# An RWKV block in f32: the LoRA products of four mixes as one group of four row tiles, their mixes in two groups, and new hand orders

## The chip, the core and the metric

The kernel runs on one core of a Trainium2 chip, all in 32-bit floats. The metric is the device time of one execution in microseconds (us), as the median of several runs. A core has TensorE (PE, matrix products into PSUM), VectorE (DVE), ScalarE (ACT), GpSimd (POOL) and SyncE (SP, here only for starting DMAs), each with its own queue of instructions that run in order; they wait for one another by semaphores. PSUM has eight banks of 512 floats in each of 128 partitions.

## The reference

64 sequences of 64 tokens with 256 features, one RWKV-6 block with 32 heads of size 8:

```
xn = layernorm(x);  sx = previous token's xn - xn
t  = tanh((xn + sx*maa_x) @ maa_w1)            # 256 -> 5 groups of 32
x5[n] = xn + sx*(maa[n] + t[n] @ maa_w2[n])    # five mixes: k, w, v, r, g
k, v, r = x5[k]@Wk.T, x5[v]@Wv.T, x5[r]@Wr.T;  g = silu(x5[g]@Wg.T)
w = exp(-exp(time_decay + tanh(x5[w]@decay_w1) @ decay_w2))
per token:  a = k (x) v;  out = r . (u*a + s);  s = a + w*s      # s is 8 x 8 a head
x = x + (groupnorm(out) * g) @ Wo.T
xn2 = layernorm(x);  xk, xr = xn2 + (previous - xn2)*ffn_maa
x = x + sigmoid(xr@ffn_Wr.T) * (relu(xk@ffn_Wk.T)**2 @ ffn_Wv.T)
```

## The kernel before, in words

The 64 sequences are cut into nine chunks, of 4, 6, then six times 8, then 6 sequences (256, 384, 512 ... 384 tokens); features lie on partitions, in two halves of 128, and tokens on the free axis. The last chunk's second half of the block is done in three parts, called 8, 9 and 10. The work of a chunk is cut into named steps, for each engine some:

- Norm and shift: `st`, `nrm` (ACT), `rd1` (POOL, a power), `T1` (PE, transposes into `pa`), `xn` (ACT), `shift` (DVE: sx and the input of the first LoRA product).
- LoRA: `W1` (PE, into `pb`), `th` (ACT, tanh), then the mixes. The first four groups of 32 rows of `th` hold the mixes k, w, v, r; mix n = 0, 1, 2, 3 is v, k, w, r, so each reads its own 32 rows of `th` and of `w2`. `X01` is the products of n = 0 and 1, both halves (`lora_half`, four products with 32 rows to contract), into `pa` and `pb`; `mix0` and `mix1` (DVE) turn them into x5. `X2` is the first halves of n = 2 and 3, into `pb`, `X3` the second halves into the same banks, so X3 waits for `mix2`, the step that reads X2; `mix3` reads X3. `X4` and `mix4` are the gate's.
- A mix is `mix_half` once for each half (L459, (product + maa) * sx) and then the addition of xn (L468, `add_xn`, on DVE), or, from chunk 2 on and for n = 1, 3, 4, an adding DMA that POOL starts (`ad1`, `ad3`, `ad4`, L363).
- Projections on PE into `pa`: `P0` (v), `P1` (k), `P3` (r), `P4` (g), each eight passes in L843 (a 32-bit product is two passes); `D1`, `D2` (decay), `CB` (L965, the bonus). ACT empties them: `v`, `k`, `thd`, `r`, `w`, `tg`.
- v goes to DRAM (`vst`, SP) and comes back repeated on the partitions (`vl0`, `vl1`, SP).
- Scan, four times q = 0 to 3: `a`q (L524, k*v), POOL's `s0`q (start state, L394), `sc`q (four scans, L534), `rs`q (times r, L542), PE's `S`q (sums into `patt`, L984, four 32-column tiles). `kv` has two buffers, so a(q) waits for S(q-2).
- Out: `BO` (L975, the bonus into `patt`), `sq` (ACT), `VR` (PE, L996), `rstd` (ACT), `gate` (DVE, L552 and L558), `WO` (PE, L850), `res` (DVE, L567), `st2`, `rd2` (POOL, L384), `nrm2`, `T2` (PE, L835), `xn2` (ACT, L792), `shift2` (DVE, L595 to L600: sx, then xr, then xk), `RR` (L850), `rr` (ACT), `KK` (L843), `kk` (ACT, L812 and L814), `Y2` (L850), `out` (DVE, L610), `ay` (POOL, an adding DMA into the output, L403). `lx` loads x, `lr` loads it again for the residual, `sx2` stores.

Each engine runs its steps in an order written out by hand, `DVE_ORDER` and so on: a pair (name, lag) stands for that step of chunk i - lag in round i; the rounds' end is replaced by a tail that names every step (`DVE_TAIL` ...). In the middle of the span DVE scans chunk c while it mixes chunk c+1 and does `gate` and `res` of chunk c-1. In DVE's order before, one round has

```
rk.1 a0.1 shift.2 bonus.1 sc0.1 gate.0 rs0.1 mix0.2 mix1.2 res.0 a1.1 a2.1 mix2.2
sc1.1 mix3.2 rs1.1 shift2.0 mix4.2 sc2.1 a3.1 rs2.1 sc3.1 rs3.1 rk.2 out.0 a0.2
```

Of the kernel before, what the change touches and what calls it, by code (L numbers as in the profile page):

```python
# [99 lines left out]


def build(nc, x, prev, s0, vecs, w1, w2, dw1, dw2, large, consts, out):

    vscr = nc.dram_tensor("v_scratch", [2, E * T], F32, kind="Internal").ap()
    with ExitStack() as ctx:
# [307 lines left out]
        def _(dve):
# [56 lines left out]
            def a_mix(c, p, n):  # L470

                dve.wait_ge(x_done, 4 * c + (4 if n == 4 else 1))
                if n == 4:

                    dve.wait_ge(pv_done, c + 1)
                elif c >= 1:
                    dve.wait_ge(pg_done if n == 0 else pk_done, c)
                src = pa if n == 0 else pb
                for a in range(HF):
                    ins = mix_half(c, n, a, src[:, a])  # L480
                ins.then_inc(mixed, 1)
                add_xn(c, n)

            def a_mix_pair(c, p, a):

                dve.wait_ge(x_done, 4 * c + 2 + a)
                if a == 0 and c >= 1:
# [3 lines left out]
                mix_half(c, 2, a, pb[:, 0])
                mix_half(c, 3, a, pb[:, 1]).then_inc(mixed, 1)
                if a == HF - 1:
                    add_xn(c, 3)

            def a_rk(c, p):
                dve.wait_ge(r_ready, c + 1)
                dve.wait_ge(k_ready, c + 1)

                dve.wait_ge(x_done, 4 * (c + 1))  # L500
# [593 lines left out]
```

## Time and profile before

| | |
|---|---|
| median of three runs | 539.96 us (539.35 to 544.64) |
| the profiled execution | 541.4 us, span 539.6 us |
| mean granted clock of TensorE | 0.918 of full |
| DVE busy | 482.4 us, 89% of the span |
| PE busy | 460.1 us (85%) |
| ACT, POOL busy | 284.3 us (53%), 91.2 us (17%) |
| 0 to 50 us | DVE busy 21.93 |
| 272 to 330 us (a full chunk) | DVE busy 57.43, PE 54.16 |
| 500 to 539.6 us | DVE busy 20.94 |

The span is the time from the first to the last instruction of the profiled execution; some time lies around it. A row of the timeline gives start, length, engine, line and operation, what it writes and reads, how many instructions are merged into it, and in brackets the engine's idle time before it with what ended that.

### The profile page before, as it was taken

What the parts mean: (1) busy time and instruction counts of PE and PEld (TensorE: products, weight loads), DVE (VectorE), ACT (ScalarE), POOL (GpSimd) and SP (SyncE); (2) the same over time, 40 slices, a digit from 0 to 9 for tenths busy, and PEclk for the clock granted to TensorE, in tenths of its full rate; (3) what the DMA queues carried; (4) which work ended last, traced back from release to release, by engine and by line L of the source; (5) the groups of instructions that cost most, each with busy time, mean ns of one, the idle gap of its engine ahead of it and who ended that gap; (6) DMA issues with size and microseconds to landing.
All of it is one profiled execution on the core that took longest, in us unless ns stands there. A gap on an engine that the chain in (4) does not pass through costs nothing.

```text
span 539.6 us, 5791 instructions
## 1 busy us (share of the span) xinstructions
PE 460.1 (85%) x1968; PEld 257.4 (48%) x1968; DVE 482.4 (89%) x530; ACT 284.3 (53%) x614; POOL 91.2 (17%) x93
## 2 busy tenths in 40 slices
PE   0786889899799988999799979999899969954857
PEld 0463554464356344654365436544465536532435
DVE  0457999999999999989999999999999999999474
ACT  5353177378526844665636852765456263633533
POOL 0001011211420041010332042113202121101020
PEclk9996989899989996998899988999799979985888
DMA  8271291688377827980798357772796069711020
GB/s 267 95 193 21 84 223 30 155 200 187 61 183 162 188 40 171 205 199 2 139 211 207 67 79 182 171 183 54 159 223 151 2 126 226 153 40 30 0 39 30
DMA packets 26726, 69.34 MB, mean 129 GB/s; under 512 B 1608, under 2 KB 19656, under 8 KB 24264
## 3 DMA queue, kind: packets, MB, share of 16 engines
q1 hardware_dynamic: 19448, 54.55, 40.6%
q0 software_dynamic: 7248, 14.42, 15.8%
q8 instruction: 16, 0.26, 0.2%
q14 instruction: 14, 0.11, 0.1%
HBM read 46.15 MB, written 12.19 MB: 108 GB/s over the span
## 4 chain that ended last, share of the span: by engine, by line
PE 51%; issue 22%; DVE 11%; ACT 9%; POOL 5%; DMA 1%; SPq 0%; DVEq 0%; ACTq 0%; POOLq 0%
PE pa L843 13%; PE pc L850 10%; PE pc L843 4%; PE patt L984 4%; PE pb L910 3%; POOL out L403 2%; PE pc L835 2%; PE pb L953 2%; DVE kv L534 2%; DVE x L459 2%; PE pa L881 2%; PE pa L938 2%; POOL rs L384 1%; ACT ob L673 1%; PE pb L869 1%
## 5 line engine op out<-in xcount | busy, mean ns | idle before, releaser
L534 DVE TENSOR_TENSOR_SCAN kv<-w_sb,kv 128x512 f32<-128x512 f32 (+2 forms) x144 | 147.1, 1083 | 0.1
L843 PE MATMUL pa<-x,large_sb 128*128 128x512 f32 (+2 forms) x288 | 129.2, 596 | 2.2 <-DVE x L468 1.7
L843 PEld LDWEIGHTS pa<-x,large_sb 128*128 128x128 f32 x288 | 59.0, 212 | 62.4 <-issue 49.4
L542 DVE TENSOR_TENSOR kv<-kv,r_sb 128x2048 f32<-128x2048 f32 (+2 forms) x36 | 73.7, 2048 | 0.4
L524 DVE TENSOR_TENSOR kv<-vrep,k_sb 128x2016 f32<-128x2016 f32 (+2 forms) x36 | 71.8, 2012 | 0.2 <-PE patt L984 0.2
L394 POOL COPY kv<-s_sb 128x32 f32<-128x32 f32 (+2 forms) x36 | 34.6, 963 | 189.8 <-PE patt L984 171.5
L881 PE MATMUL pb<-th,w_sb 32*128 32x512 f32 (+2 forms) x108 | 40.8, 681 | 18.7 <-DVE x L459 18.7
L459 DVE SCALAR_TENSOR_TENSOR x<-pb,vec_sb,sx 128x512 f32<-128x512 f32 (+2 forms) x72 | 46.1, 681 | 7.0 <-PE pb L881 4.8
L363 POOL DMA_DIRECT2D x<-xn x21 | 19.7, 936 | 177.9 <-DVE x L459 177.9
L639 ACT ACTIVATE ob<-xres 128x256 f32<-128x256 f32 x29 | 11.7, 405 | 52.1 <-DVE xres L567 52.1
L984 PE MATMUL patt<-kv,const_sb 128*32 128x512 f32 (+2 forms) x288 | 36.4, 578 | 0.1
L850 PE MATMUL pc<-large_sb,xr 128*128 128x256 f32 x120 | 30.8, 411 | 2.9 <-DVE xr L600 2.9
L850 PE MATMUL pc<-large_sb,att 128*128 128x256 f32 x120 | 29.2, 397 | 4.2 <-DVE att L558 4.2
L850 PEld LDWEIGHTS pc<-large_sb,xr 128*128 128x128 f32 x120 | 23.9, 205 | 13.2 <-DVE xr L600 5.0
L804 ACT ACTIVATE trr<-pc 128x1024 f32<-128x1024 f32 (+3 forms) x9 | 7.9, 881 | 41.9 <-PE pc L850 41.9
L850 PEld LDWEIGHTS pc<-large_sb,att 128*128 128x128 f32 x120 | 24.0, 201 | 12.0 <-DVE att L558 5.7
L850 PE MATMUL pc<-large_sb,sq 128*128 128x256 f32 x120 | 28.3, 387 | 0.5 <-ACT sq L814 0.4
L843 PE MATMUL pc<-xk,large_sb 128*128 128x512 f32 (+3 forms) x72 | 28.1, 533 | 0.4 <-ACT trr L804 0.4
L881 PEld LDWEIGHTS pb<-th,w_sb 32*128 32x128 f32 x108 | 13.2, 211 | 31.3 <-DVE x L459 25.3
L850 PEld LDWEIGHTS pc<-large_sb,sq 128*128 128x128 f32 x120 | 22.1, 190 | 9.8 <-issue 5.7
L835 PE MATMUL pc<-const_sb,ob 128*128 128x128 f32 x60 | 14.3, 409 | 13.4 <-ACT ob L673 13.4
L730 ACT ACTIVATE k_sb<-pa 128x1024 f32<-128x1024 f32 (+2 forms) x9 | 8.4, 928 | 32.2 <-PE pa L843 32.2
(128 smaller groups left out, 779.3 us busy)
## 6 DMA issues: line engine op xcount, KB each, us to landing
vrep<-v_scratch SPq DMA_DIRECT2D x12, 2048.0 KB, 13.7
x<-xn POOLq DMA_DIRECT2D x18, 512.0 KB, 7.4
vrep<-v_scratch SPq DMA_DIRECT2D x4, 1536.0 KB, 10.7
x_tok<-in_x SPq DMA_DIRECT2D x6, 512.0 KB, 9.6
v_scratch<-v_sb SPq DMA_DIRECT2D x12, 256.0 KB
xres<-in_x SPq DMA_DIRECT2D x6, 512.0 KB, 4.2
out<-xres SPq DMA_DIRECT2D x6, 512.0 KB, 13.9
out<-trr POOLq DMA_DIRECT2D x6, 512.0 KB, 7.0
```

Of the source, the lines that this page charges most:

```text
L363: pool.dma_start(x5[:, x5_slot(n), :, 0:nt], xn[:, c % 2, :, 0:nt], accum_op=ALU.add).then_inc(x5_added[n], 16)
L394: pool.tensor_copy(kv[:, q % 2, :, 0:nb, 0], s0_sb[:, half, G4 * j:G4 * (j + 1), FIRST[c]:FIRST[c] + nb]).then_inc(s0_put, 1)
L459: return dve.scalar_tensor_tensor(out=x5[:, x5_slot(n), a, 0:nt], in0=src[:, 0:nt], scalar=vec(f"maa{g}", a), in1=sx[:, a, 0:nt], op0=ALU. ...
L524: dve.tensor_tensor(kv[:, q % 2, :, 0:nb, 1:L], vv[:, G4 * j:G4 * (j + 1), :, 0:L - 1], kk, ALU.mult).then_inc(kv_ready, 1)
L534: ins = dve.tensor_tensor_scan(flat, w_sb[:, p, q % HF, 0:nb].rearrange("p b t -> p (b t)"), flat, 0.0, ALU.mult, ALU.add)
L542: dve.tensor_tensor(flat, flat, r_sb[:, p, q % HF:q % HF + 1, 0:n].broadcast_to([P, G4, n]), ALU.mult).then_inc(rs_ready, 1)
L835: ins = pe.transpose(dst[:, a, i * P:(i + 1) * P], src[:, t, a * P:(a + 1) * P], ident)
L843: ins = pe.matmul(dst[:, m, 0:n], w(a)[:, m * P:(m + 1) * P], src[:, a, :], start=(a == 0), stop=(a == HF - 1))
L850: ins = pe.matmul(product_tok(k)[:, i], src[:, a, t * P:(t + 1) * P], w(a), start=(a == 0), stop=(a == HF - 1))
L881: return pe.matmul(dst[:, 0:nt], w2_sb[rows, a * P:(a + 1) * P], th[rows, 0, 0:nt], start=True, stop=True)
L910: ins = pe.matmul(pb[:, a, f * nf:(f + 1) * nf], w24_sb[:, f, a * P:(a + 1) * P], th[:, 1, 0:nf], start=True, stop=True)
L984: ins = pe.matmul(patt[d * H:(d + 1) * H, j, 0:n], sum_k[:, half, :], kv[:, q % 2, d, 0:nb].rearrange("p b t -> p (b t)"), start=False, st ...
```

## The change

The products of n = 0 to 3 are issued together, one half of the features at a time: `XA` the first halves, `XB` the second, each four products in four row groups, into the four banks `pa[:, 0]`, `pa[:, 1]`, `pb[:, 0]`, `pb[:, 1]`. DVE's `mixA` reads all four first halves, `mixB` the second halves, with the additions of xn. XB waits until mixA has read the banks; P0, which writes `pa`, waits for the second halves of n = 0 and 1; mixA waits until P4, P1, D1 and P3 of the chunk before are done with. The orders and tails of all five engines are new, and each now has a head, written out. In the middle DVE's round becomes

```
rk.1 rs3.0 a0.1 out.-1 shift.2 bonus.1 sc0.1 gate.0 mixA.2 rs0.1 mixB.2 res.0
a1.1 a2.1 sc1.1 mix4.2 rs1.1 shift2.0 sc2.1 a3.1 rs2.1 sc3.1
```

and PE's goes from `W1 X01 BO WO S0 P0 X2 X3 T2 P1 X4 S1 RR D1 KK D2 P3 S2 Y2 T1 S3 CB VR P4` to `W1 XA BO XB WO S0 P0 X4 P1 T2 S1 D1 RR P3 KK D2 S2 Y2 T1 S3 CB VR P4`.

```diff
-PE_ORDER = [("X01", 1), ("BO", 2), ("WO", 3), ("S0", 2), ("P0", 1), ("X2", 1), ("X3", 1), ("T2", 3), ("P1", 1),
-            ("X4", 1), ("S1", 2), ("RR", 3), ("D1", 1), ("KK", 3), ("D2", 1), ("P3", 1), ("S2", 2), ("Y2", 3),
-            ("T1", 0), ("S3", 2), ("CB", 1), ("VR", 2), ("P4", 1), ("W1", 0)]
-POOL_ORDER = [("s02", 3), ("s03", 3), ("ad4", 2), ("s00", 2), ("ad0", 1), ("s01", 2), ("ad1", 1), ("rd1", 0),
-              ("ay", 4), ("rd2", 3), ("ad3", 1)]
-SP_ORDER = [("vl1", 4), ("vst", 3), ("lx", 1), ("vl0", 3), ("sx2", 5), ("lr", 4)]
+DVE_ORDER = [("a2", 3), ("sc1", 3), ("mix4", 2), ("rs1", 3), ("shift2", 4), ("sc2", 3), ("a3", 3), ("rs2", 3),
+             ("sc3", 3), ("rk", 2), ("rs3", 3), ("a0", 2), ("out", 4), ("shift", 1), ("bonus", 2), ("sc0", 2),
+             ("gate", 3), ("mixA", 1), ("rs0", 2), ("mixB", 1), ("res", 3), ("a1", 2)]
+PE_ORDER = [("W1", 1), ("XA", 1), ("BO", 2), ("XB", 1), ("WO", 3), ("S0", 2), ("P0", 1), ("X4", 1), ("P1", 1),
+            ("T2", 3), ("S1", 2), ("D1", 1), ("RR", 3), ("P3", 1), ("KK", 3), ("D2", 1), ("S2", 2), ("Y2", 3),
+            ("T1", 0), ("S3", 2), ("CB", 1), ("VR", 2), ("P4", 1)]
+POOL_ORDER = [("ay", 4), ("ad3", 1), ("rd1", 0), ("rd2", 3), ("ad4", 1), ("s03", 2), ("s00", 1), ("ad0", 0),
+              ("ad1", 0), ("s01", 1), ("s02", 1)]
+SP_ORDER = [("sx2", 7), ("vl1", 5), ("lr", 6), ("vst", 4), ("vl0", 4), ("lx", 2)]
...
-DVE_TAIL = [("rs1", 7), ("shift2", 6), ("a3", 7), ("sc2", 7), ("mix4", 8), ("rs2", 7), ("sc3", 7), ("rs3", 7),
-            ("rk", 8), ("out", 6), ("a0", 8), ("sc0", 8), ("gate", 7), ("bonus", 8), ("a1", 8), ("rs0", 8),
-            ("res", 7), ("sc1", 8), ("a2", 8), ("rs1", 8), ("sc2", 8), ("rs2", 8), ("shift2", 7), ("a3", 8),
-            ("sc3", 8), ("rs3", 8), ("gate", 8), ("gate", 9), ("out", 7), ("gate", 10), ("res", 8), ("st2", 8),
+DVE_TAIL = [("rs1", 7), ("mix4", 8), ("shift2", 6), ("a3", 7), ("sc2", 7), ("rs2", 7), ("sc3", 7), ("rs3", 7),
+            ("rk", 8), ("out", 6), ("a0", 8), ("a1", 8), ("sc0", 8), ("gate", 7), ("rs0", 8), ("sc1", 8),
+            ("bonus", 8), ("rs1", 8), ("res", 7), ("a2", 8), ("sc2", 8), ("a3", 8), ("rs2", 8), ("sc3", 8),
+            ("rs3", 8), ("shift2", 7), ("gate", 8), ("gate", 9), ("out", 7), ("res", 8), ("st2", 8),
...
-PE_TAIL = [("WO", 7), ("BO", 8), ("S0", 8), ("T2", 7), ("S1", 8), ("RR", 7), ("S2", 8), ("KK", 7), ("S3", 8),
+PE_TAIL = [("WO", 7), ("BO", 8), ("S0", 8), ("S1", 8), ("S2", 8), ("T2", 7), ("RR", 7), ("S3", 8), ("KK", 7),
            ("VR", 8), ("Y2", 7), ("WO", 8), ("WO", 9), ("WO", 10), ("T2", 8), ("T2", 9), ("RR", 8), ("T2", 10),
...
+        def rows_of(n):
+            return (pa if n < 2 else pb)[:, n % 2]
...
+            def a_mix_first(c, p):
+                dve.wait_ge(x_done, 3 * c + 1)
+                if c >= 1:
+                    dve.wait_ge(pg_done, c)
+                    dve.wait_ge(pk_done, c)
                     dve.wait_ge(d1_done, c)
                     dve.wait_ge(pr_done, c)
+                for n in range(4):
+                    ins = mix_half(c, n, 0, rows_of(n))
+                ins.then_inc(mixed, 1)
+            def a_mix_second(c, p):
+                dve.wait_ge(x_done, 3 * c + 2)
+                mix_half(c, 0, 1, rows_of(0)).then_inc(mixed, 1)
+                add_xn(c, 0)
+                mix_half(c, 1, 1, rows_of(1)).then_inc(mixed, 1)
+                add_xn(c, 1)
+                mix_half(c, 2, 1, rows_of(2))
+                mix_half(c, 3, 1, rows_of(3)).then_inc(mixed, 1)
+                add_xn(c, 3)
...
+            def x_half(c, p, a):
+                if a == 0:
+                    pe.wait_ge(th_ready, c + 1)
+                    pe.wait_ge(xn_ready, c + 1)
+                    if c >= 1:
+                        pe.wait_ge(sg_ready, c)
+                else:
+                    pe.wait_ge(mixed, 5 * c + 1)
+                for n in range(4):
+                    ins = lora_half(c, n, a, rows_of(n))
                 ins.then_inc(x_done, 1)
...
             def p_unit(c, p, n, name, freed, done):
                 wait_x5(pe, c, n)
+                if n == 0:
+                    pe.wait_ge(mixed, 5 * c + 3)
```

## Rows read from the trace of the kernel before

**Rows 1.** A stretch: busy PE, PEld, DVE, ACT, POOL (instructions), clock, DMA share, GB/s.
```profile
272.00:330.00 58.00, 54.16 (x225) 29.16 (x224) 57.43 (x54) 34.46 (x74) 14.09 (x11) 0.94 0.63 139
```

**Rows 2.** What VectorE waited for: us in total, times, longest.
```profile
DVE x L459 <- PE pb L881: 11.8, 6, 3.6
...
DVE trr L610 <- PE pc L850: 4.0, 5, 1.8
...
DVE xres L567 <- PE pc L850: 2.1, 3, 1.2
```

**Rows 3.** VectorE in order of time, 300 to 331 us.
```profile
308.21 2.28 DVE L542 TENSOR_TENSOR kv<-kv,r_sb 128x2048 f32<-128x2048 f32 x1
310.42 1.40 DVE L459 SCALAR_TENSOR_TENSOR x<-pa,vec_sb,sx 128x512 f32<-128x512 f32 x2
...
314.32 1.21 DVE L567 TENSOR_TENSOR xres<-xres,pc 128x1024 f32<-128x1024 f32 x1
315.44 4.42 DVE L524 TENSOR_TENSOR kv<-vrep,k_sb 128x2016 f32<-128x2016 f32 x2
...
321.10 4.56 DVE L534 TENSOR_TENSOR_SCAN kv<-w_sb,kv 128x512 f32<-128x512 f32 x4
```

**Rows 4.** TensorE in order of time, same stretch, columns as before.
```profile
305.94 0.69 PE L881 MATMUL pa<-th,w_sb 32*128 32x512 f32 x1 [0.89 <-ACT th L714]
...
307.86 1.98 PE L975 MATMUL patt<-bonus,const_sb 128*128 128x512 f32 x4
309.68 3.62 PE L850 MATMUL pc<-large_sb,att 128*128 128x256 f32 x16
313.23 1.06 PE L984 MATMUL patt<-kv,const_sb 128*32 128x512 f32 x8
...
317.85 1.13 PE L881 MATMUL pb<-th,w_sb 32*128 32x512 f32 x4
321.24 2.08 PE L881 MATMUL pb<-th,w_sb 32*128 32x512 f32 x4 [2.26 <-DVE x L459]
324.00 1.97 PE L835 MATMUL pc<-const_sb,ob 128*128 128x128 f32 x8 [0.69 <-ACT ob L673]
```

**Rows 5.** TensorE in chunk 1's X01, in order of time.
```profile
49.28 0.84 PE L881 MATMUL pa<-th,w_sb 32*128 32x384 f32 x1
...
49.92 0.84 PE L881 MATMUL pa<-th,w_sb 32*128 32x384 f32 x1
```

**Rows 6.** Stretches of 1 us; clock third from the end (columns of rows 1).
```profile
321.00:322.00 1.00, 0.76 (x2) 0.50 (x4) 1.00 (x2) 0.97 (x5) 0.00 (x0) 0.50 1.03 135
327.00:328.00 1.00, 1.00 (x2) 0.34 (x1) 1.00 (x1) 0.46 (x1) 0.74 (x2) 0.59 0.26 102
```

**Rows 7.** TensorE near the end, in order of time.
```profile
496.67 6.29 PE L850 MATMUL pc<-large_sb,xr 128*128 128x256 f32 x16 [2.90 <-DVE xr L600]
...
504.16 3.67 PE L843 MATMUL pc<-xk,large_sb 128*128 128x512 f32 x8 [0.42 <-ACT trr L804]
```

**Rows 8.** GpSimd (POOL) in order of time, 314 to 321 us.
```profile
314.69 0.86 POOL L363 DMA_DIRECT2D x<-xn  x1 [17.34 <-DVE x L459]
...
316.26 3.63 POOL L403 DMA_DIRECT2D out<-trr  x1
319.80 1.16 POOL L384 TENSOR_TENSOR rs<-var,neg_half 128x4 f32<-128x4 f32 x1
```

**Rows 9.** VectorE near the end, in order of time.
```profile
493.85 0.19 DVE L595 TENSOR_TENSOR sq<-prev_sb,xn 128x16 f32<-128x16 f32 x1 [0.57 <-ACT xn L792]
...
503.15 1.76 DVE L542 TENSOR_TENSOR kv<-kv,r_sb 128x1536 f32<-128x1536 f32 x1
515.26 0.61 DVE L552 SCALAR_TENSOR_TENSOR att<-patt,vec_sb,rstd 128x128 f32<-128x128 f32 x2 [10.35 <-ACT rstd L784]
```

**Rows 10.** ScalarE (ACT) in order of time: a norm's last step, and the end.
```profile
326.01 1.45 ACT L792 ACTIVATE xn<-pc,vec_sb 128x512 f32<-128x512 f32 x2 [2.06 <-PE pc L835]
...
509.39 1.02 ACT L812 ACTIVATE sq<-pc 128x1024 f32<-128x1024 f32 x1
```

More of the change, by code:

```diff
@@ new lines @@
+POOL_ORDER = [("ay", 4), ("ad3", 1), ("rd1", 0), ("rd2", 3), ("ad4", 1), ("s03", 2), ("s00", 1), ("ad0", 0),
+              ("ad1", 0), ("s01", 1), ("s02", 1)]
+SP_ORDER = [("sx2", 7), ("vl1", 5), ("lr", 6), ("vst", 4), ("vl0", 4), ("lx", 2)]
+SUBS = 3
+DVE_TAIL = [("rs1", 7), ("mix4", 8), ("shift2", 6), ("a3", 7), ("sc2", 7), ("rs2", 7), ("sc3", 7), ("rs3", 7),
+            ("rk", 8), ("out", 6), ("a0", 8), ("a1", 8), ("sc0", 8), ("gate", 7), ("rs0", 8), ("sc1", 8),
+            ("bonus", 8), ("rs1", 8), ("res", 7), ("a2", 8), ("sc2", 8), ("a3", 8), ("rs2", 8), ("sc3", 8),
+            ("rs3", 8), ("shift2", 7), ("gate", 8), ("gate", 9), ("out", 7), ("res", 8), ("st2", 8),
+            ("gate", 10), ("res", 9), ("st2", 9), ("nrm2", 8), ("res", 10), ("nrm2", 9), ("st2", 10),
+            ("shift2", 8), ("nrm2", 10), ("shift2", 9), ("shift2", 10), ("out", 8), ("out", 9), ("out", 10)]
@@ new lines @@
+POOL_TAIL = [("ad4", 8), ("s02", 7), ("s03", 7), ("s00", 8), ("ay", 6), ("s01", 8), ("s02", 8), ("s03", 8),
+             ("rd2", 7), ("ay", 7), ("rd2", 8), ("ay", 8), ("rd2", 9), ("rd2", 10)]
+SP_TAIL = [("vl1", 6), ("vst", 7), ("sx2", 5), ("lr", 6), ("vl0", 7), ("vl1", 7), ("vst", 8), ("sx2", 6),
+           ("vl0", 8), ("vl1", 8), ("lr", 7), ("sx2", 7), ("lr", 8), ("sx2", 8)]
+DVE_HEAD = [("shift", 0), ("mixA", 0), ("mixB", 0)]
+PE_HEAD = [("T1", 0), ("W1", 0), ("XA", 0), ("XB", 0), ("P0", 0), ("P1", 0), ("D1", 0), ("X4", 0), ("P3", 0),
+           ("T1", 1), ("D2", 0), ("P4", 0), ("CB", 0), ("W1", 1)]
@@ L65 @@
+ACT_HEAD = [("st", 0), ("nrm", 0), ("xn", 0), ("th", 0), ("st", 1), ("nrm", 1), ("v", 0), ("k", 0), ("thd", 0)]
+POOL_HEAD = [("rd1", 0), ("ad0", 0), ("ad1", 0), ("rd1", 1), ("ad3", 0)]
+SP_HEAD = [("lx", 0)]
+LAGS = 7
 ADDED = (0, 1, 3, 4)
-MIXED = {0: 1, 1: 2, 3: 4, 4: 5}
+MIXED = {0: 2, 1: 3, 3: 4, 4: 5}
 FILL = 2
@@ L93, in part, with schedule @@
     return LAST, (k - LAST) * n, n
-def schedule(table, tail):
-    return [(name, i - lag) for i in range(NCH + LAGS) for name, lag in table
-            if 0 <= i - lag < NCH and (name, i - lag) not in tail] + tail
+def schedule(head, table, tail):
+    return head + [(name, i - lag) for i in range(NCH + LAGS) for name, lag in table
+                   if 0 <= i - lag < NCH and (name, i - lag) not in head + tail] + tail
 def build(nc, x, prev, s0, vecs, w1, w2, dw1, dw2, large, consts, out):
@@ L468, in add_xn, with a_mix_gate @@
                     dve.tensor_tensor(dst, dst, xn[:, c % 2, :, 0:nt], ALU.add).then_inc(x5_ready[n], 1)
[L470 to L487, printed above, removed]
+            def a_mix_first(c, p):
[3 more added lines that the diff above has]
+                    dve.wait_ge(pk_done, c)
                     dve.wait_ge(d1_done, c)
                     dve.wait_ge(pr_done, c)
[L491 to L494, printed above, removed]
+                for n in range(4):
[10 more added lines that the diff above has]
+                add_xn(c, 3)
+            def a_mix_gate(c, p):
+                dve.wait_ge(x_done, 3 * c + 3)
+                dve.wait_ge(pv_done, c + 1)
+                for a in range(HF):
+                    ins = mix_half(c, 4, a, pb[:, a])
+                ins.then_inc(mixed, 1)
+                add_xn(c, 4)
             def a_rk(c, p):
@@ L498, in a_rk @@
                 dve.wait_ge(k_ready, c + 1)
[L500 removed]
+                dve.wait_ge(x_done, 3 * (c + 1))
                 n = extent(c)[1]
@@ L621, in _ @@
                 "shift": a_shift, "rk": a_rk, "bonus": a_bonus,
-                **{f"mix{n}": (lambda c, p, n=n: a_mix(c, p, n)) for n in (0, 1, 4)},
-                "mix2": lambda c, p: a_mix_pair(c, p, 0), "mix3": lambda c, p: a_mix_pair(c, p, 1),
+                "mixA": a_mix_first, "mixB": a_mix_second, "mix4": a_mix_gate,
                 **{f"a{q}": (lambda c, p, q=q: b_products(c, p, q)) for q in range(NQ)},
```

52 lines of the change are left out of this document (15 added, 37 removed).

## The prediction

> **What bounds the kernel now.** I read the busy time by stretches first, then what VectorE (DVE) waits for, then one cycle of it beside TensorE (PE), and at last the end of the span. In a stretch with a full chunk DVE is busy 57.43 of 58 us and PE 54.16 [rows 1]. So DVE sets the period: the reader should see that microseconds taken off PE count there only where DVE waits for PE. It waits little. Over the whole span the waits of `out` for the last product are 4.0 us in five pieces, 0.31 of it in the last microseconds; those of `res` for Wo are 2.1 in three, those of the mixes for a LoRA product 11.8 in six [rows 2]. The head holds nearly all of the last kind: the longest, 3.6, is chunk 0's first mix, and chunk 1's first starts only when X01 ends at 50.77 [rows 2, 5].
>
> PE is not far from the bound: it idles 0.89 us before X01 for tanh and 2.26 before X3 for the mixes; after the second its clock is down (next part), X3 takes 2.08 us where X2 took 1.13, and the transposes T2 take 1.97 [rows 4]. `out` is then late by 0.4 to 1.8 us in a full chunk.
>
> **The change, part by part.**
>
> *PE work.* Before: X01 is four products in pairs, from 305.94 to the start of BO at 307.86, 1.92 us; X2 1.13; X3 2.08 with its idle 2.26. After: XA and XB, each four products with four row groups and four banks. A pair of two-pass products takes 1.13 at full clock, whose shape (8 passes in two slots) is also that of the eight passes of a sum, which go to four column tiles and take 1.06 in all [rows 4]. So I take 1.13 for XA and for XB, at worst 1.92 if only pairs overlap. PE loses 1.92 + 1.13 + 2.08 - 2.26 = 2.9 us a full chunk. Nearly none of it is on the path of DVE.
> The page TensorE: Matmul & The Clock Gate of the Trainium skill (Part 3, measured speedup) gives a four-row packing of K=32, N=512 3.07 times the speed of one after another; by it XA takes 4 / 3.07 = 1.3 times one product, at 1.13 for one some 1.5 us, an estimate from that page; XB would end 0.4 later and the sum be 1.5 us larger where `res` waits. No row here shows row groups four deep.
>
> *DVE work.* The same instructions; the sum per period stays. What goes: the waits of `out`, which now stands after a0, one product (2.2 us, half of 4.42 [rows 3]) later, while PE has less before it; and the small waits of `res` and mix2 in the middle. Of the waits in [rows 2] I take all 3.7 of `out` that lie before the end, 0.6 of `res` and 0.6 of the mixes: -4.9 us.
> The page TensorEngine Tiling of the Trainium skill (PSUM Bottleneck) says that tiling speeds up TensorE but not the evacuation of PSUM, which may then be the bottleneck. The trace agrees: two mixes take 1.40 us on DVE [rows 3] against two slots for four products on PE. By that rule alone the gain is zero, which is what the sum gives for this part without the waits.
>
> *Head.* XA of chunk 1 does in two slots what X01 does in four. The slots were 0.64 us apart there (49.28 to 49.92) [rows 5], and the mix waited for the last of them. So XA ends 1.3 us sooner, and P0 of that chunk now stands behind all the first halves and the adds, off DVE's path as long as v comes back from DRAM in time. In chunk 0 the gain of two slots is eaten, since P0, and so v, waits for XB and for the mixes of n=0 and 1 (some 2 us later); the load of v is now issued ahead of the x load, which gives part of that back. I take -1.0, bounds -2 and +1.5.
>
> *A new wait: XB for mixA, and WO behind it.* This is the main term. XB overwrites the four banks, so it waits until DVE has read them all. Ahead of mixA on DVE stands gate, which ends where rs0 began, 308.21 [rows 3]. mixA is four halves, twice 1.32 (pair to pair), 2.65 us: to 310.9. PE in the meantime has XA (1.13 from 305.94) and BO (1.8) and is through at 308.9. It idles 2.0 us, and up to 3 where PE, with less work, comes earlier. Queued behind XB are WO, S0, P0, X4. Who waits: `res`, which needs WO, is due on DVE after rs0 (2.2) and mixB (3.9, as from 310.42 to 314.32 [rows 3]), that is 6.1 after mixA. At full clock XB 1.1 and WO 3.6 [rows 4] end at 4.7: covered by 1.4. At half clock they don't. In the cycle shown the clock was down at 321 to 322 (0.50), after an idle 2.26 us that began at 318.98, and came back in the microsecond 327 to 328 (0.59) [rows 6]: some 6.2 us from the start of X3. These are the two levels, 1.2 and 2.4 GHz. Put the same 6.2 us on XB: XB takes 2.08; until 6.2 WO does (6.2 - 2.1) / 2 = 2.05 of its 3.6; it ends at 6.2 + 1.55 = 7.75. `res` is 1.6 late, call it 1.45 as the idle starts a little before. Nothing for chunk 2 (WO a half chunk), 0.5 at most for chunk 3. Bounds: 0 if the clock holds, 2.2 if it stays down (16 passes took 6.29 after an idle of 2.90 [rows 7]). Of the old waits before X3 not each was followed by so long a spell, so I count four of the five full chunks: +5.8.
>
> *POOL and T2.* `rd2`, the power for the second norm, now stands behind s02 (which waits for S0, so for WO), ay, ad3 and rd1. Now it stands behind ad1, rd1 and ay: from 314.69 to 319.80 those held POOL, and T2 began 9.7 us after `res` began (314.32, 324.00) [rows 8, 3, 4]. shift2 is due on DVE after two products, a scan, a mix and a read, 1.1 + 4.3 + 4.5 + 1.3 + 2.2 = 13.4 us after `res` starts. POOL: s02 may start 1 us after `res`, takes 1 to 2; then 5.1 for the three as above, 1.2 for rd2; then 3.0 for the norm on ACT (320.96 to 324.00), 1.0 for T2, 1.4 for xn2 [rows 8, 4, 10]: 13.7 to 14.7. So it is 0.3 to 1.3 late; I take 0.3 in five chunks: +1.5, bounds 0 and 6. P1 waits for the DMA of its add, 4.85 after mixA plus landing; T2 stands behind it, but not later than this.
>
> *Order of SP.* lx goes behind vl0, lr and sx2 behind the next v loads. DVE never waited for a v or x load after the head [rows 2], and I leave that at nothing; if the v load came 3 us late in each chunk it would be the product a0 that waits.
>
> *Tail.* shift2 of chunk 7 goes from before a3 of chunk 8 to behind its last read rs3; on PE, RR of 7 stands ahead of S3 of 8. Before: shift2 began at 493.85 after idling 0.57, RR at 496.67 took 6.29, KK started at 504.16, the last read of DVE ended at 504.9, and the gate came at 515.26 after idling 10.35 [rows 7, 9]. After: DVE reaches the end of rs3 without shift2's 4.0 and without two waits (1.18 for `res`, 0.57): 499.1. From there: 2.82 to RR, 7.49 from RR's start to KK's start, 3.67 KK, then the two steps of kk on ACT and the norm's two, which took 515.26 - 509.39 = 5.87 [rows 9, 10]. Sum 19.85: the gate at 518.95, 3.7 later. With RR at full clock (3.7 instead of 6.29) 1.1 later. KK's 3.67 stands between S3 and the variance product as well, which is why no step of it can be passed. I take +3.5. What follows the gate is the same work.
>
> *Sum.* -1.0 - 4.9 + 5.8 + 1.5 + 3.5 = +4.9 us. The profiled execution took 541.4 (span 539.6 and 1.8 around it), so 546.3; it was 1.4 above the median 539.96, which the forecast is to be held against: 544.9, say 545. The three runs spread over 5 us, so a change within 1% (5.4 us) can hardly be told from none.
>
> **The rivals.**
> *The clock holds, and PE's relief shows.* For it: PE idles in fewer pieces, and the short clock spells of the old kernel cost DVE nothing. Against it: an idle of 2 us before XB in each chunk, like the one before X3. Then `res` and shift2 are on time and the tail loses 1.1: -1.0 - 4.9 + 1.1 = -4.8, 535; with the head's better bound 534. This is the other side.
> *POOL decides.* rd2 behind s02 and ay makes shift2 wait 1.3 us and T1, CB and `bonus` after it some more: 5 to 6 us over the sum, 550. For it: the issue of ay alone took 3.63 beside rd1 [rows 8]. It decides from 13.4 us after `res`.
> *The change doesn't do what it says: only pairs overlap.* X01 started its two products within 0.01 us and the next two 0.54 later; the same in XB would put WO back by 0.8 in each of five chunks: +4, 549.
>
> **How the numbers follow.** My forecast, spells of low clock that make `res` late, 0.42, its own range 541 to 549. The clock holds 0.33 (530 to 538). POOL 0.15, pairs only 0.10 (547 to 556). Faster by over 1% is below 534.6: two thirds of the second case, 0.23. Slower by over 1% is above 545.4: somewhat under half of the first case, and the last two, 0.43. Within 0.34. The range 532 to 554 leaves out the ends.
>
> **What would show it.** Right: XA and XB of 8 passes in 1.1 us each; an idle of 2 to 3 us before XB; a PE clock of 0.50 right after it; `res` on DVE idle 1 to 2 us on WO in most full chunks; no wait of `out`; the last gate some 19 us after the last read. Wrong: a clock of 1.00 through WO; `sq` or `kv` products of DVE waiting for ACT or a DMA in full chunks; a period under the 57.4 us that DVE is busy in a stretch of 58, which would mean that its instructions became faster.

## The result, and the profile after

The changed kernel took 545.1 us (median) beside 541.8 for the kernel before, ratio 1.0081 [1.0054, 1.0107]. Timed again beside the later experiments it took 543.56 beside 541.61, ratio 1.0041 [1.0014, 1.0069]. It is slower by some 0.6%. The forecast was 545.0, and that agreement is worth little: below, its largest term is absent and three others have taken its place; and it was counted from 539.96, the median of three runs, where the kernel before, timed beside the changed one, took 541.8. As a change it was +5, and +3.3 and +2.0 were measured.

The profiled execution took 543.78 us, its span 542.0, 2.4 longer than before. A full chunk by stretches, and what VectorE waited for in the whole span:

```profile
272.00:330.00 58.00, 51.62 (x224) 27.36 (x224) 57.06 (x54) 34.31 (x75) 8.87 (x11) 0.97 0.67 146
```

```profile
DVE att L569 <- ACT rstd L800: 14.9, 1, 14.9
...
DVE x L469 <- PE pb L897: 5.7, 3, 2.8
DVE th L519 <- ACT r_sb L758: 4.5, 6, 0.8
...
DVE kv L541 <- issue: 3.7, 2, 3.0
DVE bonus L526 <- PE pb L979: 1.8, 1, 1.8
```

Against [rows 1, 2]: PE is busy 2.5 us less in the stretch and its clock is higher, 0.97 for 0.94. The waits of `out` and `res` for a product are gone from the middle. Three kinds of wait are new: in the full chunks `th` (the product rk of r and k) for r, where before 3.76 of its 4.0 us stood in chunk 0; and in the head `bonus` for CB, and the product a0 (L541) for something the profile calls "issue". Of what a0 waits for in the kernel, that leaves the load of v. The last gate waits 14.9 for its rstd, before 10.35 [rows 9]. One wait looks worse than it is: the gate's mix of chunk 0 waits 8.13 where it waited 2.04, but rk, next on DVE, now waits 0.81 for 3.76, and counted from the first shift it starts only 0.1 later (23.80 for 23.67).

Where the time went is read by one instruction that has the same neighbours in both kernels, the first of `shift` (L442 before, L452 after), chunk by chunk:

| start of, us | before | changed | changed again (e8) |
|---|---|---|---|
| shift of chunk 1 | 40.95 | 41.45 | 41.17 |
| shift of chunk 4 | 179.22 | 181.91 | 181.68 |
| shift of chunk 8 | 413.58 | 414.04 | 414.20 |
| last operation of DVE | 536.46 | 539.29 | 539.48 |

So the changed kernel loses 2.7 us up to chunk 4 (2.46 in the second profile), gains 2.2 in the four full chunks after that (1.8), and loses 2.4 after chunk 8's shift (2.4).

One full chunk on PE, columns as in [rows 4], and the clock in stretches of 1 us:

```profile
306.78 0.70 PE L897 MATMUL pa<-th,w_sb 32*128 32x512 f32 x2 [0.89 <-ACT th L730]
306.79 0.70 PE L897 MATMUL pb<-th,w_sb 32*128 32x512 f32 x2
307.31 0.59 PE L897 MATMUL pa<-th,w_sb 32*128 32x512 f32 x2
307.32 0.59 PE L897 MATMUL pb<-th,w_sb 32*128 32x512 f32 x2
307.85 1.98 PE L989 MATMUL patt<-bonus,const_sb 128*128 128x512 f32 x4
311.78 0.70 PE L897 MATMUL pa<-th,w_sb 32*128 32x512 f32 x2 [1.95 <-DVE x L469]
...
312.86 3.72 PE L866 MATMUL pc<-large_sb,att 128*128 128x256 f32 x16
...
331.33 1.93 PE L998 MATMUL patt<-kv,const_sb 128*32 128x512 f32 x8 [1.95 <-DVE kv L559]
```

```profile
311.00:312.00 1.00, 0.22 (x4) 0.22 (x8) 1.00 (x3) 0.00 (x0) 0.00 (x0) 1.00 0.00 0
313.00:314.00 1.00, 1.00 (x5) 0.90 (x6) 1.00 (x2) 0.00 (x0) 0.00 (x0) 1.00 0.00 0
...
332.00:333.00 1.00, 1.00 (x8) 0.00 (x0) 0.96 (x2) 0.00 (x0) 0.00 (x0) 0.50 1.02 233
```

The four products of XA start within 0.02 us in each of two slots, and BO starts 1.07 after XA: four row tiles do run at once. XB comes after an idle of 1.95 us and at full clock; WO behind it takes 3.72 and ends at 316.6. On DVE `res` then starts without a wait, and the wait of this cycle is elsewhere:

```profile
291.34 1.22 DVE L519 TENSOR_TENSOR th<-r_sb,k_sb 128x1024 f32<-128x1024 f32 x1 [0.80 <-ACT r_sb L758]
...
317.74 1.21 DVE L584 TENSOR_TENSOR xres<-xres,pc 128x1024 f32<-128x1024 f32 x1
```

```profile
288.28 1.02 ACT L828 ACTIVATE sq<-pc 128x1024 f32<-128x1024 f32 x1 [5.84 <-PE pc L859]
289.34 1.06 ACT L830 ACTIVATE sq<-sq 128x1024 f32<-128x1024 f32 x1
290.30 1.00 ACT L758 ACTIVATE r_sb<-pa 128x1024 f32<-128x1024 f32 x1
```

```profile
281.21 3.60 PE L859 MATMUL pa<-x,large_sb 128*128 128x512 f32 x8
284.65 3.60 PE L859 MATMUL pc<-xk,large_sb 128*128 128x512 f32 x8
```

The product of r (P3, into pa) is through at 284.8. ScalarE is idle then, but its next step is kk, which needs KK, the product after P3. So r is taken out 5.5 us after it is there, and rk waits 0.8 us for it in each full chunk.

In the head, PE and DVE:

```profile
41.04 3.60 PE L859 MATMUL pa<-x,large_sb 128*128 128x256 f32 x8 [2.80 <-ACT xn L711]
...
55.65 5.46 PE L859 MATMUL pa<-x,large_sb 128*128 128x384 f32 x8 [1.51 <-DVE x L469]
```

```profile
45.54 0.69 DVE L526 TENSOR_TENSOR bonus<-v_sb,pb 128x512 f32<-128x512 f32 x1 [1.83 <-PE pb L979]
...
78.35 1.73 DVE L541 TENSOR_TENSOR kv<-vrep,k_sb 128x1512 f32<-128x1512 f32 x1 [3.05 <-issue]
```

CB of chunk 0 stands behind P4, which waits 2.8 for xn and then runs at half clock (3.60), and `bonus` waits for CB. P0 of chunk 1 waits for mixB to leave pa and takes 5.46 at half clock, where before it took 3.34 from 53.72; v is stored 4.0 us later than before (61.98 for 57.94), and a0 of chunk 1 waits 3.05 us for its load. Without that wait it would have started at 75.30, before at 75.75.

The tail, on PE and on DVE, beside [rows 7, 9]:

```profile
501.71 5.41 PE L866 MATMUL pc<-large_sb,xr 128*128 128x256 f32 x16 [4.46 <-DVE xr L617]
507.05 0.85 PE L998 MATMUL patt<-kv,const_sb 128*32 128x384 f32 x8
508.32 3.67 PE L859 MATMUL pc<-xk,large_sb 128*128 128x512 f32 x8 [0.42 <-ACT trr L820]
...
514.19 3.72 PE L866 MATMUL pc<-large_sb,sq 128*128 128x256 f32 x16 [0.91 <-ACT sq L830]
```

```profile
517.90 0.61 DVE L569 SCALAR_TENSOR_TENSOR att<-patt,vec_sb,rstd 128x128 f32<-128x128 f32 x2 [14.92 <-ACT rstd L800]
```

The last read ends at 498.91, the gate comes 19.0 us later.

### The profile page after: what moved, and what is told of

Same layout as the page of the kernel before. It is cut to its first block, busy times and chain, and to the rows that moved or that the text cites. A ratio compares the mean times of both kernels' runs of the same rounds, so it can differ in the third digit from the quotient of the medians.

```text
span 542.0 us, 5792 instructions
## 1 busy us (share of the span) xinstructions
PE 435.2 (80%) x1968; PEld 244.3 (45%) x1968; DVE 481.0 (89%) x530; ACT 283.3 (52%) x614; POOL 80.0 (15%) x93
## 4 chain that ended last, share of the span: by engine, by line
DVE 41%; PE 21%; issue 19%; DMA 11%; ACT 5%; POOL 2%; SPq 1%; DVEq 0%; ACTq 0%; POOLq 0%
DVE kv L551 12%; DVE x L469 8%; DVE kv L559 7%; DMA vrep<-v_scratch 6%; PE pa L859 6%; DVE kv L541 5%; PE pc L866 4%; DMA v_scratch<-v_sb 3%; PE pc L859 3%; DMA out<-xres 2%; DVE att L569 2%; PE patt L998 2%; DVE bonus L526 2%; DVE sx L453 2%; PE pa L952 1%
## 5 line engine op out<-in xcount | busy, mean ns | idle before, releaser
L859 PE MATMUL pa<-x,large_sb 128*128 128x512 f32 (+2 forms) x288 | 123.6, 575 | 15.7 <-ACT v_sb L738 7.8
L541 DVE TENSOR_TENSOR kv<-vrep,k_sb 128x2016 f32<-128x2016 f32 (+2 forms) x36 | 71.8, 2015 | 3.7 <-issue 3.7
L998 PE MATMUL patt<-kv,const_sb 128*32 128x512 f32 (+2 forms) x288 | 39.7, 630 | 24.7 <-DVE kv L559 24.6
L373 POOL DMA_DIRECT2D x<-xn x21 | 24.1, 1147 | 199.0 <-DVE x L469 199.0
L404 POOL COPY kv<-s_sb 128x32 f32<-128x32 f32 (+2 forms) x36 | 23.7, 736 | 178.6 <-PE patt L998 159.8
L469 DVE SCALAR_TENSOR_TENSOR x<-pb,vec_sb,sx 128x512 f32<-128x512 f32 (+2 forms) x54 | 34.5, 682 | 8.1 <-PE pb L922 8.1
L897 PE MATMUL pa<-th,w_sb 32*128 32x512 f32 (+2 forms) x72 | 19.6, 624 | 23.2 <-DVE x L469 15.7
L469 DVE SCALAR_TENSOR_TENSOR x<-pa,vec_sb,sx 128x512 f32<-128x512 f32 (+2 forms) x36 | 23.9, 686 | 5.7 <-PE pb L897 5.7
L828 ACT ACTIVATE sq<-pc 128x1024 f32<-128x1024 f32 (+3 forms) x9 | 7.9, 881 | 39.2 <-PE pc L859 39.2
L569 DVE SCALAR_TENSOR_TENSOR att<-patt,vec_sb,rstd 128x512 f32<-128x512 f32 (+3 forms) x22 | 12.1, 591 | 14.9 <-ACT rstd L800 14.9
L998 PEld LDWEIGHTS patt<-kv,const_sb 128*32 128x32 f32 x288 | 6.0, 113 | 36.0 <-DVE kv L559 29.5
```

The costliest lines, as they stand in the source:

```text
L373: pool.dma_start(x5[:, x5_slot(n), :, 0:nt], xn[:, c % 2, :, 0:nt], accum_op=ALU.add).then_inc(x5_added[n], 16)
L404: pool.tensor_copy(kv[:, q % 2, :, 0:nb, 0], s0_sb[:, half, G4 * j:G4 * (j + 1), FIRST[c]:FIRST[c] + nb]).then_inc(s0_put, 1)
L469: return dve.scalar_tensor_tensor(out=x5[:, x5_slot(n), a, 0:nt], in0=src[:, 0:nt], scalar=vec(f"maa{g}", a), in1=sx[:, a, 0:nt], op0=ALU. ...
L541: dve.tensor_tensor(kv[:, q % 2, :, 0:nb, 1:L], vv[:, G4 * j:G4 * (j + 1), :, 0:L - 1], kk, ALU.mult).then_inc(kv_ready, 1)
L569: ins = dve.scalar_tensor_tensor(out=att[:, j, span(k)], in0=patt[:, j, span(k)], scalar=vec("gn_w", j), in1=rstd[:, span(k)], op0=ALU.mul ...
L859: ins = pe.matmul(dst[:, m, 0:n], w(a)[:, m * P:(m + 1) * P], src[:, a, :], start=(a == 0), stop=(a == HF - 1))
```

## The experiments

**Four parts, each alone.** e1 changes one place of ScalarE's order:

```diff
-("rr", 3), ("kk", 3), ("r", 1), ("w", 1)
+("rr", 3), ("r", 1), ("kk", 3), ("w", 1)
```

> The changed kernel, with ScalarE's step r of a chunk put ahead of kk of the chunk two before. Theory of the queue: in the changed kernel VectorE's rk waits 0.8 us in each full chunk because r stands behind kk, and kk waits for PE's KK, which follows P3; with r first rk does not wait, and kk is not later because KK ends 3.4 us after P3. Five full chunks with that wait (0.5, 0.8, 0.8, 0.8, 0.8): 3.7 us faster than the changed kernel, so about 541.4 and a ratio near 1.001 to the kernel before; period of a full chunk 57.2 instead of 58.03. Rival: VectorE's round is held by something else as well (the product for out, or r itself from P3), and the wait turns up at another instruction: ratio stays at 1.008, period 58.0.

541.95 us, ratio 1.0005 [0.998, 1.0031]. In its trace r comes right behind P3, and no rk waits in a full chunk:

```profile
285.37 1.02 ACT L758 ACTIVATE r_sb<-pa 128x1024 f32<-128x1024 f32 x1 [2.41 <-PE pa L859]
```

A full chunk takes 57.13 us (shift at 299.09, then 356.22) for 58.03 in the changed kernel. The wait for r is caused by its place behind kk. This trace has a new wait further on, 1.02 us of a0 for the load of v at 411.14, and gains nothing from chunk 7's shift to chunk 8's (58.22). e4, e7 and e10 have 0.5 to 0.9 at the same place and the two profiles of the changed kernel none, so it does not come from this edit alone.

e2 moves CB in the head of PE:

```diff
-("D2", 0), ("P4", 0), ("CB", 0), ("W1", 1)]
+("D2", 0), ("CB", 0), ("P4", 0), ("W1", 1)]
```

> The changed kernel, with PE's head in the order D2, CB, P4 of chunk 0 instead of D2, P4, CB. Theory of the head: bonus of chunk 0 waits 1.83 us for CB, which stands behind P4, and P4 waits 2.8 us for xn of chunk 1; everything of chunk 1 follows, v's way through DRAM too, so a0 of chunk 1 comes 1.8 us sooner and the whole with it: ratio near 1.0045. Rival: the v load of chunk 1 is late for a reason of its own (the DMA queues) and lands at the same time whatever the mixes do: a0 of chunk 1 still starts at 78.3 and the ratio stays at 1.008.

540.74 us, ratio 1.0012 [0.9978, 1.0046]. The wait of `bonus` is gone, and from the gate's mix of chunk 0 to a0 of chunk 1 there are 42.23 us (35.30 to 77.53) for 44.38 (33.97 to 78.35), 2.15 less. But the same stretch took 43.04 in the second profile of the changed kernel (33.70 to 76.74, e8 below), because the wait for v at its end was shorter there, 1.77. Without that wait, which is 2.93 in e2, it is 39.30 for 41.33 and 41.27: CB's place costs 2.0. The ratio came out below the expected 1.0045, which its interval just reaches. The profile is of an execution 4.3 us above the median of its run.

e3 rearranges the tail:

In this notation `S3.8` is step S3 of chunk 8; only the stretch that changes is shown.

```diff
 PE    -T2.7 RR.7 S3.8 KK.7 VR.8 Y2.7 WO.8 WO.9 WO.10
       +T2.7 S3.8 VR.8 RR.7 KK.7 WO.8 WO.9 Y2.7 WO.10
 ACT   -rr.7 sq.8 kk.7 rstd.8
       +sq.8 rstd.8 rr.7 kk.7
 DVE   -gate.9 out.7 res.8 st2.8 gate.10 res.9 st2.9 nrm2.8 res.10 nrm2.9
       +gate.9 gate.10 res.8 st2.8 res.9 st2.9 nrm2.8 out.7 nrm2.9 res.10
 POOL  -rd2.7 ay.7 rd2.8 ay.8 rd2.9
       +rd2.7 rd2.8 rd2.9 ay.7 ay.8
```

> The changed kernel with another end: S3 and the variance product of chunk 8 ahead of RR and KK of chunk 7 on PE, WO of the first two parts ahead of Y2 of chunk 7, sq and rstd ahead of rr and kk on ScalarE, the third gate and the first norms ahead of out of chunk 7 on VectorE, and POOL's powers ahead of its adding DMA. Theory of the queue: the 14.9 us that VectorE waits for rstd of the last chunk are RR (5.4), KK (3.7) and the steps of kk that stand ahead; the last read ends at 498.9, so rstd is ready 7 us later, at 506, the gate at 506 instead of 517.9; then PE's RR, KK, kk, Y2 bound the end and of the 11.9 us some 4 to 6 are left: ratio 0.997 to 1.001. Rival: the end is bound by the chain RR, KK, Y2 and what follows it whatever stands around it: less than 1 us, ratio 1.007.

542.58 us, ratio 1.0019 [0.9986, 1.0052], a little above the expected range.

```profile
506.74 0.61 DVE L569 SCALAR_TENSOR_TENSOR att<-patt,vec_sb,rstd 128x128 f32<-128x128 f32 x2 [3.92 <-ACT rstd L800]
...
535.07 0.42 DVE L627 SCALAR_TENSOR_TENSOR trr<-trr,pa 128x256 f32<-128x256 f32 x1 [5.84 <-PE pa L866]
```

The gate comes 11.2 us earlier, the end only 2.0: from chunk 8's shift to the last operation 123.35 us (413.90 to 537.25) for 125.25. The rest is given back in waits for PE behind the gate, the longest 5.84.

e10 has only the first half of that, S3 and VR ahead of RR on PE, sq and rstd ahead of rr on ACT:

> The changed kernel with two moves in the tail alone: PE has S3 and VR of the last chunk ahead of RR and KK, ScalarE has sq and rstd of the last chunk ahead of rr and kk. Y2, WO, the gates and out stay where they are. If the late S3 is what the tail costs, gate 8 starts 11 us earlier (its wait 14.9 falls to about 4) and the end comes with it by 2 to 3 us: ratio 0.999 to 1.002. Rival, what follows (Y2 of chunk 7 behind kk, WO behind Y2, out of 7 ahead of the last gate) sets the end whatever gate 8 does: the gain at the gate is all given back, ratio 1.004 to 1.008.

544.49 us, ratio 1.0057 [1.0025, 1.0089]: the rival is right. From chunk 8's shift to the last operation there are 124.67 us (414.49 to 539.16) for 125.25.

```profile
506.67 0.61 DVE L569 SCALAR_TENSOR_TENSOR att<-patt,vec_sb,rstd 128x128 f32<-128x128 f32 x2 [3.26 <-ACT rstd L800]
...
520.36 1.22 DVE L627 SCALAR_TENSOR_TENSOR trr<-trr,pc 128x1024 f32<-128x1024 f32 x1 [11.26 <-PE pc L866]
```

The wait at the gate has moved, nearly whole, to `out` of chunk 7 behind it, which needs Y2.7. So the gate does not set the end of the changed kernel; by the rows it is shift2.7, RR, KK and Y2 in a row.

**The clock, made to fall.** e4 lengthens PE's idle before XB:

```diff
-("XA", 1), ("BO", 2), ("XB", 1), ("WO", 3)
+("XA", 1), ("XB", 1), ("BO", 2), ("WO", 3)
```

> The changed kernel with XB ahead of BO on PE, so that PE idles once for 3.8 us ahead of XB instead of 1.95, and WO comes 1.8 later. It asks what the forecast had wrong: whether an idle of that kind brings the clock down and makes res late. If it does: clock 0.50 in the microseconds after XB's start, XB 2.1 us, BO and WO at half speed, res of a full chunk waits 3 to 5 us, ratio 1.035 to 1.05. If the clock holds: XB 1.1, BO 1.8, WO 3.6 after mixA, 6.6 us, res due at 6.1, so 0.4 late, ratio 1.01 to 1.013.

564.92 us, ratio 1.0405 [1.0354, 1.0456]. On PE, by the clock, and on DVE:

```profile
323.24 1.22 PE L897 MATMUL pa<-th,w_sb 32*128 32x512 f32 x2 [3.87 <-DVE x L469]
...
325.26 3.78 PE L989 MATMUL patt<-bonus,const_sb 128*128 128x512 f32 x4
```

```profile
322.00:323.00 1.00, 0.00 (x0) 0.00 (x0) 1.00 (x2) 0.20 (x1) 0.00 (x0) 0.55 0.00 0
...
328.00:329.00 1.00, 1.00 (x3) 0.48 (x2) 1.00 (x3) 0.00 (x0) 0.63 (x2) 0.54 0.00 0
329.00:330.00 1.00, 1.00 (x7) 0.87 (x6) 0.38 (x1) 0.00 (x0) 0.47 (x2) 1.00 0.35 66
```

```profile
332.54 1.22 DVE L584 TENSOR_TENSOR xres<-xres,pc 128x1024 f32<-128x1024 f32 x1 [3.15 <-PE pc L866]
```

This is the chain that the forecast described, only after an idle twice as long: the clock at its lower level, 1.2 GHz, from about 322.1 to 328.9, some 6.8 us, XB and BO up to twice as long, `res` late by 3.1 in four full chunks and 4.1 in a fifth. BO's new place ahead of WO has a share in this: by the expectation's sum `res` would be 0.4 late at full clock.

**Grouping and orders apart.** e5 keeps the grouped products and goes back to the orders of the kernel before on all engines; e9 keeps the old products (X01, X2, X3) in the new orders.

```diff
 e5  PE   XA.1 BO.2 WO.3 S0.2 XB.1 P0.1 T2.3 P1.1 ...      (lags as in the tables)
     DVE  ... rs0.2 mixA.1 res.3 mixB.1 a1.2 a2.2 sc1.2
 e9  PE   W1.1 X01.1 BO.2 X2.1 X3.1 WO.3 S0.2 P0.1 X4.1 ...
     DVE  ... gate.3 mix0.1 mix1.1 rs0.2 mix2.1 mix3.1 res.3 a1.2
```

> The grouped products in two halves of the features, but on every engine the order of the kernel before (no heads, old tails); only the steps of the mixes take the place of the old ones (DVE rs0, mixA, res, mixB, a1; PE XA, BO, WO, S0, XB, P0). It tells the grouping from the orders. Theory A, the grouping itself gains and the new orders spend it: the PE work of the mixes shrinks by 2.9 us a chunk, the waits of out (3.7 in all) and of the mixes (0.6) go, head and tail stay as before, rk does not wait for r: ratio 0.985 to 0.995. Theory B, grouping needs the new order: mixB now stands behind res, PE idles over 3 us before XB as in the run with XB ahead of BO, the clock falls to half, and v comes later: ratio 1.005 to 1.03.

569.88 us, ratio 1.0537 [1.0492, 1.0582]: theory B, and more than its upper end. The long idle is not where the expectation put it. XB follows S0 without an idle and is through at 333.7, and mixB waits only 0.32 for it. But P0 now stands right behind XB, with nothing in between, and cannot have its bank until mixB has read it:

```profile
332.53 0.70 PE L896 MATMUL pa<-th,w_sb 32*128 32x512 f32 x2
...
336.56 5.37 PE L858 MATMUL pa<-x,large_sb 128*128 128x512 f32 x8 [2.89 <-DVE x L468]
347.06 1.97 PE L850 MATMUL pc<-const_sb,ob 128*128 128x128 f32 x8 [5.13 <-ACT ob L688]
348.82 4.81 PE L858 MATMUL pa<-x,large_sb 128*128 128x512 f32 x8
```

```profile
333.74 0.75 DVE L468 SCALAR_TENSOR_TENSOR x<-pa,vec_sb,sx 128x512 f32<-128x512 f32 x1 [0.32 <-PE pb L896]
```

In the changed kernel WO and S0 stand between XB and P0, 4.6 us of work, and fill that time. So the idle that I had expected before XB stands before P0, and a second one, 5.13, before T2: on POOL rd2 stands behind ad1, which starts at 336.71, when mixB has done its part. The products after both run partly at half clock. shift2 waits 1.66 for its norm and `out` 1.77 for Y2 in most full chunks.

> The kernel before with its own mix products (X01, X2, X3 in two banks at a time), in the new orders: X2 and X3 stand on PE where XB does, mix0 and mix1 where mixA, mix2 and mix3 where mixB, the heads as in the changed kernel. Together with the run of the grouping in the old orders (1.054) it tells whether either part gains by itself. Theory A, grouping and orders are one change: X3 must wait for the eviction of mix2 (0.7 us and the way) while WO, S0 and P0 stand behind, PE idles 2 us and 1.4 us more, the clock falls and res is late: ratio 1.02 to 1.05. Theory B, the gain of the middle (2.1 us) is the orders' and the grouping is idle: 1.002 to 1.010.

599.66 us, ratio 1.1032 [1.0984, 1.1079], twice what I had put as the worst.

```profile
349.77 1.13 PE L887 MATMUL pb<-th,w_sb 32*128 32x512 f32 x4 [2.37 <-DVE x L465]
353.29 2.08 PE L887 MATMUL pb<-th,w_sb 32*128 32x512 f32 x4 [2.39 <-DVE x L465]
355.30 4.92 PE L856 MATMUL pc<-large_sb,att 128*128 128x256 f32 x16
```

```profile
355.42 1.41 DVE L465 SCALAR_TENSOR_TENSOR x<-pb,vec_sb,sx 128x512 f32<-128x512 f32 x2 [2.18 <-PE pb L887]
...
360.26 1.22 DVE L573 TENSOR_TENSOR xres<-xres,pc 128x1024 f32<-128x1024 f32 x1 [3.43 <-PE pc L856]
```

Two idles in a row, clock down, WO 4.92 instead of 3.72 (6.37 in another chunk), mix3 waits 2.18 for X3 in the middle, and `res` 3.4 to 5.2 in each full chunk. So neither part gains by itself: either alone costs 5 or 10%, both together 0.6%.

**The v load in the head.** e7 puts the load of the tokens behind the second v load:

```diff
-("sx2", 7), ("vl1", 5), ("lr", 6), ("vst", 4), ("vl0", 4), ("lx", 2)]
+("sx2", 7), ("vl1", 5), ("lx", 3), ("lr", 6), ("vst", 4), ("vl0", 4)]
```

> The changed kernel with one move on SP's queue: the load of the tokens (x_tok, 512 KB) behind the second of the two v loads instead of between them. If the long wait before a0 of chunk 1 (3.05 us in the changed kernel, 0.6 more in chunk 2) is the v loads sharing the DMA engines with the tokens, the wait falls by 0.6 (the issue) to 1.5 us and the time by as much: ratio 1.004 to 1.007. Rival, the first v load is what a0 waits for and it is ahead of the tokens anyway: nothing changes, 1.007 to 1.010; or the tokens come late for the norms: over 1.010.

> The changed kernel itself, timed beside the others on the same chip, so that the three edits are read against it and not only against the kernel before. Expected 1.0081 again, 1.006 to 1.010. If it is lower by 0.003 or more, the gains read from the first four runs were partly the chip's, not the edits'.

e7 took 544.35 us, ratio 1.0056 [1.0024, 1.0089]; e8, the changed kernel itself, 543.56 us and 1.0041. The move gains nothing that can be told. e7's wait at a0 of chunk 1 is 2.19, but e8's is 1.77 where the first profile had 3.05, so this wait varies between executions by as much as was expected from the move; and e7's profile is of an execution 5 us above its median, with 12.5 us of wait at the gate's mix of chunk 0. The run does not settle what part of v's way is the late one. Between its two timings the changed kernel itself differs by 0.4%, more than the 0.003 that e8's expectation had named: part of what e1 to e3 seem to gain in their ratios was not the edits'. Against the changed kernel they can be read to no better than that; the traces carry them.

**All three edits at once.** e6 is e1, e2 and e3 together:

> The changed kernel with the three edits of the first runs at once: r and w work of ScalarE ahead of kk, CB ahead of P4 in the head, and the tail with S3 and VR ahead of RR and KK. By the traces of the three alone they gain 2.7 us of the full chunks' rk waits, about 2.1 at the first long a0 of chunk 1, and 2.0 at the end; they lie in different stretches. Theory A, they add: 545.1 - 6.8, ratio 0.992 to 0.996 of the kernel before. Rival, the head's gain is taken back by the wait for the v load in chunk 2 and the tail's by PE, so that no more than the best of them stays: 0.998 to 1.001.

536.82 us, ratio 0.9924 [0.989, 0.9957]: 6.7 us under e8, timed beside it. It beats the changed kernel and the one before. The three traces summed to 6.8, but the parts agree less well than the sum. Beside the first profile of the changed kernel, e6's gains 3.8 up to chunk 4's shift (178.13 for 181.91), 1.1 in the four full chunks after that (230.99 for 232.13) and 0.7 behind them (124.55 for 125.25), 5.6 in all. A full chunk takes 57.2 (292.47 to 349.68), except where the load of v is late, which takes back 2.2 of the middle:

```profile
405.81 2.26 DVE L541 TENSOR_TENSOR kv<-vrep,k_sb 128x2016 f32<-128x2016 f32 x1 [2.21 <-issue]
```

## Why the prediction was right in its number and wrong in its reasons

**The main term failed.** "XB for mixA, and WO behind it" was +5.8 and is 0. Its parts held: XB does wait for mixA, after an idle of 1.95 us (forecast 2.0), with BO, XB and WO as long at full clock as put. What failed is the one step "put the same 6.2 us on XB". I took the idle of 2.26 before X3 [rows 4] as enough reason for the clock to fall after 2.0 as well. It stayed at its upper level through XB and WO, 1.07 and 3.72 us in the cycle shown, and WO took 3.72 behind XB in all five full chunks; a clock of 1.00 through WO was the forecast's own sign of being wrong. `res` was on time. The 6.2 was itself read a little short: with 0.59 in the microsecond 327 to 328 the clock came back at 327.8, 6.6 after X3's start [rows 6, 4]. e4 shows that the chain and about the size of the spell were right: given 3.87 of idle, the clock falls, for 6.8 us, 5.7 of them behind XB's start, and `res` waits 3.15. The rival "the clock holds" was the true case for the middle, and I had given it 0.33.

**POOL and T2**, +1.5, is 0: shift2 never waited in a full chunk. rd2 started at 323.21, and T2 at 328.28 was in time. The sum took ay at the 3.63 of [rows 8]; here it took 1.31.

**The old waits**, -4.9: they went, as forecast. But 3.7 came back in the same stretch as rk's waits for r, five of them, which the forecast does not have at all. I had gone through the queues of PE, POOL and SP past each moved step, and not through ACT's, where kk stands ahead of r. The change moved P3 on PE from behind KK to in front of it and left r behind kk on ACT. Undoing that gives 2.7 us from chunk 3's shift to chunk 7's (e1: 227.24 for 229.97), and 2.5 up to chunk 8's.

**The head**, -1.0 with bounds -2 and +1.5, is +2.7 by shift of chunk 4, 0.4 of it present at the first shift. XA did end sooner: chunk 1's first mix starts at 50.12 for 50.82 before, though `bonus` ahead of it had waited 1.8. (That rk of chunk 1 starts 1.65 earlier, at 73.23, says little, since rs3 now stands behind it.) Two things took it back. CB behind P4 costs 2.0 (e2). And "off DVE's path as long as v comes back in time" named the condition but gave it no price: P0 of chunk 1, late and at half clock, stored v 4.0 us later, and a0 waited 3.05 (1.77 in e8). That the late store is what a0 waited for is read from the trace; no run changed it, and e7 did not settle it. The forecast's own sign for this, "it would be the product a0 that waits", stands under the order of SP, where it was put at nothing.

**The tail**, +3.5, is +2.4 from chunk 8's shift on and 2.6 at the gate. The step counts were right: last read 498.91 (forecast 499.1), gate 19.0 us later (19.85), with RR at 5.41 instead of 6.29, part of it at half clock. But the step behind them, that the end comes later because the gate does ("What follows the gate is the same work"), is wrong: e10 takes S3 forward, the gate comes 11 us earlier and the end hardly moves. By the rows what sets the end is shift2.7 behind the last read with RR, KK and Y2 of chunk 7 in a row behind it, for which `out` of chunk 7 and the last WO wait. That putting shift2.7 back would mend it is argued from this chain and was not run.

**The other rivals.** Only pairs overlapping is refuted: XA took two slots of 0.53. By the page TensorE: Matmul & The Clock Gate of the Trainium skill (Part 3) I had worked out 1.5 us for it; BO starts 1.07 after XA, and the measurement decides. Most of the difference was my own reading: I had put 1.13 for one product, which is the time of a pair. Eight passes of 512 columns one after the other took 3.60 here (P3), so one product of two passes takes 0.90. With that, the figure 3.07 of that page of the Trainium skill gives 1.2 us for the four together, an estimate. The rule of the page TensorEngine Tiling of the Trainium skill (PSUM Bottleneck), that tiling leaves the evacuation as it is, would give no gain. The trace agrees as far as it goes: the two mixes of [rows 3] are 1.40 in the changed kernel too. What moved the time in e1 to e4 and e6 was order alone.

In sum: forecast -1.0 - 4.9 + 5.8 + 1.5 + 3.5 = +4.9; measured between the two traces +2.7 (head), -2.2 (full chunks), +2.4 (tail), which is +2.8 before rounding, as at the last operation. The medians say +2 to +3.3. That the forecast's time was met is luck. It had 5.8 too much for the clock, 1.5 for POOL and 1.1 for the tail, and 3.7 too little for the head and 3.7 for rk's waits; most of that cancels, and the low median that it was counted from did the rest.

## What to carry to other kernels

When a step moves on one engine, list for every engine what stands right behind the product that moved with it: the cost here was on ACT, an idle engine that waited in order for the wrong product. An early gate or an early product is worth what the next wait of the same chain leaves of it; take the latest wait away first, then look again. Two halves of a change may each cost 5 to 10% and cost next to nothing together, so the order has to be costed for the new grouping, not for either by itself.

## What the runs showed of the hardware that was not expected

The length of one idle does not say whether TensorE's clock falls. In the changed kernel 1.95 us before XB left it at 1.00 (311.78), with one of 0.89 before XA; 1.95 before the second sums (331.33), with idles of 1.20 and 0.42 before them, was followed by 0.50. In e9 the same X2 after the same idle of 2.37 us took 1.13 in two full chunks, 1.45 in one and 2.08 in another. In the head P1 of chunk 0 took 1.97 in two executions of the changed kernel and in e3, e6 and e10, and 3.75 in e1, e2, e4 and e7, with nothing changed before it; the gate's mix waited 8 or 9.9 accordingly, and 12.5 in e7, where the products behind P1 were slow too. What decides between them stays open.
